# Two graph convolutions on one core: the step loops unrolled, four chunks of edges to a step, the rows of the feature tiles taken in another order

## The reference

```python
deg  = segment_sum(1, src);  dinv = deg > 0 ? rsqrt(max(deg, 1)) : 0
norm = -dinv[src] * dinv[dst]
prop(h)    = segment_sum(h[src] * norm[:, None], dst)
conv(h, l) = h @ Wl_0 + prop(h) @ Wl_1 + bl
h   = leaky_relu(layer_norm(conv(x, 1)) * gamma + beta, 0.01)
out = layer_norm(x + conv(h, 2))
```

## Time and profile before

| | us |
|---|---|
| timed, median of 3 runs (lowest, highest) | 2444.04 (2441.00, 2445.28) |
| profiled execution, span from the first to the last instruction | 3370.7 |
| TensorE busy in it | 2065.1 |
| GpSimd busy | 1700.9 |
| VectorE busy | 1544.4 |
| ScalarE busy | 505.3 |

### The profile page before, as it was taken

How to read it: one execution, slowest core, us unless ns; L and a number is a source line. 1 busy time by engine, 2 the same in 40 slices (tenths; PEclk the granted TensorE clock), 3 DMA queues, 4 the chain that set the end, 5 groups by cost and what they waited for, 6 DMA issues and landing times.

```text
span 3370.7 us, 41016 instructions
## 1 busy us (share of the span) xinstructions
PE 2065.1 (61%) x7250; PEld 963.6 (29%) x7251; DVE 1544.4 (46%) x3507; ACT 505.3 (15%) x1030; POOL 1700.9 (50%) x1725
## 2 busy tenths in 40 slices
PE   6836576665665665665764656565565656555655
PEld 5712232222222322232331222222222222222222
DVE  6754444444444444544443444444444434444444
ACT  5920111111111211111230000000000000000000
POOL 0156554545555554655526545554545445554543
PEclk6558887887887878887876878787777777878778
DMA  6376565655555555655646555565555555555554
GB/s 215 133 259 181 150 174 155 173 159 160 164 167 168 159 165 157 181 159 167 182 132 200 166 158 171 166 177 155 167 159 164 155 158 165 161 165 162 159 159 122
DMA packets 215109, 559.98 MB, mean 166 GB/s; under 512 B 48100, under 2 KB 49760, under 8 KB 214948
## 3 DMA queue, kind: packets, MB, share of 16 engines
q0 software_dynamic: 133120, 436.31, 45.9%
q10 hardware_dynamic: 44676, 81.73, 7.2%
q1 hardware_dynamic: 37152, 40.21, 3.6%
HBM read 493.08 MB, written 64.18 MB: 165 GB/s over the span
## 4 chain that ended last, share of the span: by engine, by line
PE 30%; another core or an unknown queue 26%; issue 25%; DVE 8%; ACT 5%; DVEq 3%; ACTq 1%; DMA 1%; POOL 1%; SPq 0%; POOLq 0%
PE bank L749 16%; PE bank L710 10%; DVE acc L947 6%; PE bank L668 2%; ACT work L556 2%; ACT feat L564 1%; DVEq L923 1%; PE bank L727 1%; PE bank L655 1%; DVEq L947 1%; DVE onehot L923 1%; POOL ring L444 1%; ACT work L546 1%; ACTq L528 0%
## 5 line engine op out<-in xcount | busy, mean ns | idle before, releaser
L444 POOL DMA_INDIRECT ring<-table,index x1664 | 1672.6, 1005 | 1466.5 <-SPq L393 952.1
L947 DVE SCALAR_TENSOR_TENSOR acc<-bank,down,acc 128x512 f32 x928 | 696.9, 751 | 1219.6 <-PE bank L710 709.8
L710 PE MATMUL bank<-ring,onehot 128*128 x3712 | 920.3, 406 | 306.0 <-issue 148.1
L749 PE MATMUL bank<-wA,feat 128*128 128x512 f32 x784 | 547.6, 863 | 804.2 <-ACT feat L564 748.2
L923 DVE TENSOR_SCALAR onehot<-count_h,dst_c,neg_tile 128x128 f16<-128x128 f16 x1856 | 489.2, 329 | 490.1 <-issue 487.6
L710 PEld LDWEIGHTS bank<-ring,onehot 128*128 128x128 f16 x3712 | 380.6, 103 | 865.6 <-issue 515.3
L749 PEld LDWEIGHTS bank<-wA,feat 128*128 128x128 f32 x784 | 212.0, 285 | 1084.9 <-ACT feat L564 774.3
L727 PE MATMUL bank<-wB,base_in 128*128 128x512 f32 x784 | 353.6, 594 | 0.0
L546 ACT ACTIVATE work<-acc 128x512 f32 (+1 forms) x98 | 61.7, 630 | 1747.4 <-issue 1039.3
L727 PEld LDWEIGHTS bank<-wB,base_in 128*128 128x128 f32 x784 | 149.5, 191 | 155.8 <-issue 142.1
L564 ACT ACTIVATE feat<-bank 128x512 f32<-128x512 f32 x98 | 58.5, 597 | 845.4 <-remote 828.7
(11 more groups left out here) (118 smaller groups left out, 689.6 us busy)
## 6 DMA issues: line engine op xcount, KB each, us to landing
ring<-table,index POOLq DMA_INDIRECT x1664
base_in<-feat ACTq DMA_DIRECT2D x98, 256.0 KB
feat<-feat SPq DMA_DIRECT2D x49, 256.0 KB, 2.9
table<-work SPq DMA_DIRECT2D x49, 256.0 KB, 3.1
feat<-feat ACTq DMA_DIRECT2D x49, 256.0 KB
table<-work ACTq DMA_DIRECT2D x49, 256.0 KB
feat<-in_x ACTq DMA_DIRECT2D x48, 256.0 KB
out<-work ACTq DMA_DIRECT2D x48, 256.0 KB
```

The lines of the kernel that those rows point to most:

```text
L444: nc.gpsimd.indirect_dma_start(out=ring[:, at * ROW:(at + 1) * ROW], out_offset=None, in_=table[l], in_offset=bass.IndirectOffsetOnAxis(ap ...
L710: last = nc.tensor.matmul(bank[u % SUM_BANKS][:, :], onehot[:, u, j, :], ring[:, bass.ds(at, D)], start=j + half == 0, stop=j + half == GROUP)
L749: last = nc.tensor.matmul(to[:, :], feat[:, 2 + tile_slot, c * P:(c + 1) * P], wA[:, c * D:(c + 1) * D], start=False, stop=c == KB - 1)
L947: nc.vector.scalar_tensor_tensor(tile_of(acc, tile[u]), bank[u % SUM_BANKS][:, :], col(down[:, l, :], tile[u]), tile_of(acc, tile[u]), ALU ...
```

## The change

- `GROUP` is 4: 208 groups, 208 + 48 = 256 steps a layer with 8 matmuls each. The ring has 4 groups of 4 chunks (the same bytes), and a slot is given back when the group two places earlier is used up and the newer one has landed (`FREE_LAG` 2).
- All loops over steps, groups and gathers are unrolled. GpSimd's gathers lose `bounds_check` and take their indices from one SBUF tensor for the whole layer; the copies of indices by SyncE go.
- The one-hots of two steps (8 matrices) are one `tensor_tensor` with operands repeated by stride 0, from a table `rel` of target minus tile start. `rel` is made in the prologue: 28 comparisons on VectorE (`pick`), 14 fp32 matmuls on TensorE in visits 34 to 47, and an addition. The tables of the steps are built on VectorE behind the first eight low parts rather than behind the last.
- The sums are added unscaled (`tensor_tensor`). The scale is applied by the turn, a matmul of the sums with a scaled identity (`diag`). The copy `staged` goes, and so does the copy of the layer's result back to `acc` in layer 1.
- A visit on TensorE is in another order: first the turns of older tiles, then the dense part of the tile before (`W0`, bias, `W1`), then the turn of its own sums. The lags are 1, 2 and 3. Visits stand behind single steps, about 5.2 steps apart; VectorE's are 3 steps later.
- The load of `W1` (layer 1) moves from the start to behind the picks.

```diff
-    GROUP = 2
-    GROUPS = -(-E // (GROUP * P))
+    GROUP = 4
+    GROUPS = -(-E // (2 * P)) * 2 // GROUP
...
-    RING = UNROLL
-    FREE_LAG = 4
+    BLOCK = 8 // GROUP
+    HOTS = BLOCK * GROUP
+    RING = 16 // GROUP
+    FREE_LAG = RING // 2
...
+    WALK_VISIT = HIST_VISITS + 7
+    PICK_VISIT = HIST_VISITS + 10
...
-    LAG_STATS, LAG_NORMAL, LAG_HIDDEN, LAG_LEAKY, LAG_BACK, LAG_LOW = 1, 2, 3, 4, 5, 6
+    SPACING = STEPS * 256 // TILES
+    FIRST_PLACE = -(-STEPS // TILES) + 8 // GROUP
+    STATS_LATER = -(-STEPS // TILES) // 2
+    LAG_SUMS, LAG_NORMAL, LAG_HIDDEN = 1, 2, 3
...
+                for g in range(GROUPS):
+                    k = g % RING
+                    wait(pool, ring_free, GROUPS * l + g - RING + 1)
+                    for j in range(GROUP):
+                        at = k * GROUP + j
+                        c = g * GROUP + j
+                        nc.gpsimd.indirect_dma_start(
+                            out=ring[:, at * ROW:(at + 1) * ROW], out_offset=None, in_=table[l],
+                            in_offset=bass.IndirectOffsetOnAxis(ap=index[:, c:c + 1], axis=0)
+                        ).then_inc(ring_landed[k], 16)
...
+            def pick_part(m):
+                half, b = m // EDGE_BLOCKS, m % EDGE_BLOCKS
+                at = slice(half * HALF, (half + 1) * HALF)
+                return nc.tensor.matmul(pick_banks[half][:, 0:HALF_COLS].rearrange("p (n j) -> p n j", j=GROUP),
+                                        edge_f[1][:, b * P:(b + 1) * P], pick[b][:, at, :],
+                                        start=b == 0, stop=b == EDGE_BLOCKS - 1)
...
+                if PICK_VISIT <= it.least < PICK_VISIT + 2 * EDGE_BLOCKS:
+                    pe.wait_ge(pick_ready, 1)
+                    last = pick_part(it.least - PICK_VISIT)
...
+            def visit(it, steps, l):
+                if l == 0 and it.within(LAG_NORMAL, TILES + LAG_NORMAL):
+                    k = it.back(LAG_NORMAL)
+                    pe.wait_ge(normed_ready, k.n + 1)
+                    pe.wait_ge(sums_moved, k.n + 2 if k.least + 1 < TILES else TILES)
+                    turn(normed[k.slot], bank[TURN_BANK], normed_turned)
+                if l == 0 and it.within(LAG_HIDDEN, TILES + LAG_HIDDEN):
+                    k = it.back(LAG_HIDDEN)
+                    pe.wait_ge(hidden_ready, k.n + 1)
+                    wait(pe, split1_done, k.n)
+                    turn(feat[:, k.slot, :], bank[BACK_BANK], back_done)
+                if it.within(LAG_SUMS, TILES + LAG_SUMS):
+                    k = it.back(LAG_SUMS)
...
+                    dense(to, base_in[:, k.slot, :], wB, True)
+                    nc.tensor.matmul(to[:, :], ones_b[0:BIAS_PARTS, :], bias_parts[:, l * D:(l + 1) * D],
+                                     start=False, stop=False)
+                    pe.wait_ge(sums_moved, TILES * l + k.n + 1)
+                    dense(to, sums_t[k.slot], wA, False).then_inc(out_done, 1)
+                if it.within(0, TILES):
+                    pe.wait_ge(sums_added, STEPS * l + steps)
+                    pe.wait_ge(diag_ready, TILES * l + it.n + 1)
...
+                    for c in range(KB):
+                        last = nc.tensor.matmul(bank[TURN_BANK][:, c * P:(c + 1) * P],
+                                                acc[:, bass.ds(it.n * D + c * P, P)], diag[:, it.slot, :],
+                                                start=True, stop=True)
+                    last.then_inc(sums_turned, 1)
...
-            looped(dve, low_rows, 0, TILES - 1, 8)
-            straight(low_rows, TILES - 1, TILES, 8)
+            straight(low_rows, 0, 8, 8)
...
+            for b in range(EDGE_BLOCKS):
+                for j in range(GROUP):
+                    last = nc.vector.tensor_scalar(pick[b][:, :, j], group_f, (j - b * P) / GROUP, part_group[:, 0:1],
+                                                   ALU.add, ALU.is_equal)
+            last.then_inc(pick_ready, 1)
...
+            looped(dve, low_rows, 8, TILES - 1, 8)
+            straight(low_rows, TILES - 1, TILES, 8)
...
+                nc.vector.tensor_tensor(onehot[:, b % 2, :, :], count_h[:, :].unsqueeze(1).to_broadcast([P, HOTS, P]),
+                                        rel[:, b * HOTS:(b + 1) * HOTS].unsqueeze(2).to_broadcast([P, HOTS, P]),
+                                        ALU.is_equal).then_inc(onehots_ready, 1)
```

More of the change, by code:

```diff
@@ L276, in load_early, with place, visits_late @@
                 skip_runtime_bounds_check_because="early is a constant less a maximum between zero and it")[1][0]
[L278 to L295, removed]
-            straight(period, 0, 2, 1)
-            looped(eng, period, 2, PERIODS - 1, 1)
-            straight(period, PERIODS - 1, PERIODS, 1)
-        def visits_late(eng, early, drain, visit):
+        def place(v):
+            return min(STEPS, FIRST_PLACE + (v * SPACING >> 8))
+        def visits_late(eng, early, drain, visit, unrolled=False):
             def one(it):
@@ new lines, in _ @@
+            for l in range(2):
+                for n in range(STEPS):
+                    if n % BLOCK == 0:
+                        entry = nc.values_load_multi_w_load_instructions(
+                            step_u[0:1, n * ENTRY:(n + BLOCK) * ENTRY], engines=[mybir.EngineType.PE], min_val=0,
+                            max_val=RING * GROUP * ROW - D, skip_runtime_bounds_check_because=WALK_FITS)[1]
+                    step(l, n, entry[n % BLOCK * ENTRY:(n % BLOCK + 1) * ENTRY])
+                    for v in range(TILES):
+                        if place(v) == n + 1:
+                            with pe.If(early > v):
+                                visit(numbered(v), n + 1, l)
+                visits_late(pe, early, (LAG_HIDDEN, LAG_SUMS)[l], lambda it, steps: visit(it, steps, l), True)
@@ L861, in _ @@
+            assert all(place(v) == FIRST_PLACE + (v * SPACING >> 8) for v in range(BOUNDS)) and place(BOUNDS) == STEPS
+            link(nc.vector.tensor_scalar(place_i[:, 0:1], part_i[:, :], SPACING, None, ALU.mult))
             link(nc.vector.tensor_scalar(place_i[:, 1:2], place_i[:, 0:1], 8, None, ALU.arith_shift_right))
             link(nc.vector.tensor_copy(place_f[:, 0:1], place_i[:, 1:2]))
-            link(nc.vector.tensor_tensor(place_f[:, 1:2], place_f[:, 0:1], part[:, :], ALU.add))
@@ L898, in _ @@
+            for b in range(2):
+                hots(0, b)
             dve.wait_ge(s_bias, 32)
@@ new lines, in visit1 @@
+            def visit1(it, _):
+                if it.within(LAG_NORMAL, TILES + LAG_NORMAL):
+                    shifts(1, it.back(LAG_NORMAL))
+                if it.within(LAG_SUMS, TILES + LAG_SUMS):
+                    k = it.back(LAG_SUMS)
+                    s = k.slot
+                    dve.wait_ge(out_done, TILES + k.n + 1)
+                    dve.wait_ge(s_resid[s], 16 * (k.turn + 1))
+                    nc.vector.tensor_tensor(tile_of(acc, k.n), bank[OUT_BANK + s][:, :], feat[:, 2 + s, :], ALU.add
+                                            ).then_inc(resid_added, 1)
+                    dve.wait_ge(resid_added, k.n + 1)
+                    wait(dve, shift_ready, TILES + k.n - 1 if k.least > 1 else 0)
+                    statistics(1, k.n, s, tile_of(acc, k.n))
```

679 lines of the change are left out of this document (333 added, 346 removed).

## The result

The changed kernel takes 2627.03 us (median of 4 runs, 2626.48 to 2627.96) beside 2444.18 us (4 runs): ratio 1.0753, interval [1.0738, 1.0768]. It is 183 us slower. The forecast was 2470 us, with a range from 2330 to 2560.

The account below looks back on a forecast made before the run. GpSimd's gather issue was taken as the bound from end to end, 2435 us. Adding 12 and 10 (prologue), 2 (between layers) and 8 (end) gave 2467, with part of 9 us left over 2470 us; range 2330 to 2560.

Parts of the forecast that it names:

- What is saved beside the path ... Is the cover there?: VectorE, ScalarE and TensorE work off GpSimd's path: savings worth 0, TensorE keeps up with 18.6 of 22.2 us a tile.
- fourth rival: TensorE becomes the bound, its 18.6 us a tile growing to 23 at a granted clock of 0.8; 2570 us, chance 13%.
- three signs of being wrong: Gathers' distance moves over 0.02 us, GpSimd waits over 30 us for slots, or the first gather comes before 210 us.
- The gathers' distance: GpSimd's 1664 gathers stay 1.305 us apart without the bounds check; 0 us.
- first rival: Gathers get shorter without their check; a twentieth gives 84 us, a tenth 167: 2386 to 2303 us, chance 22%.
- third rival: VectorE's long one-hots hold up GpSimd's gathers, some 70 to 190 us; 2600 us, chance 7%.
- second rival: The recorder is part of the 1.305 us between gathers; at 1.25 us the changed kernel takes 2384 us, chance 12%.
- The stalls belong to the recorded execution: The profile's 914 us of stalls for ring slots are hardly in the timed run, which is GpSimd's issue throughout.
- Between them: From layer 1's last gather to layer 2's first: 40 us against 38, taken as +2 us (-8 to +10).
- VectorE's 12 us: Prologue: picks and table instructions on VectorE make the first gather 12 us late (8 to 16).
- TensorE's 10 us: Prologue: fp32 picks in TensorE's visits, 12 x 0.9 us, add 10 us.
- fifth rival: The prologue hides: ScalarE's slack is larger and TensorE's picks fit in; 2445 us, chance 6%.

Follow-up runs that it names:

- e9: Control: the kernel before with the two counts in its waits written as `max`, on a chip of 2443 us; 2442.93 us, ratio 1.0003.
- e1: The changed kernel with the bounds check put back on its gathers; 2627.46 us, ratio 1.0742.
- e2: The changed kernel with each one-hot built by its own `tensor_scalar` instead of one `tensor_tensor` for eight; 2627.82 us, ratio 1.0746.
- e3: The changed kernel with two numbers a step for TensorE instead of nine, the other offsets added up in registers; 2502.05 us, ratio 1.0236.
- e11: The changed kernel with as many numbers for TensorE, but the offsets as int32 in a load of their own; 2501.7 us, ratio 1.024.
- e10: The kernel before without the bounds check on its gathers, on a chip of 2443 us; 2358.84 us, ratio 0.9656.
- e4: The changed kernel with both one-hots by `tensor_scalar` and two numbers a step for TensorE; 2412.27 us, ratio 0.9876.
- e12: The changed kernel with one-hots by `tensor_scalar`, two numbers a step and the bounds check back, on a chip of 2443 us; 2477.62 us, ratio 1.0144.
- e13: The changed kernel with two numbers a step and one-hots as eight short `tensor_tensor` that keep two tensor inputs; 2428.33 us, ratio 0.9939.
- the second set: Four follow-up kernels run on another chip, where the kernel before itself takes 3455.38 us.
- e8: The changed kernel with one-hots by `tensor_scalar`, two numbers a step and the bounds check back, on the chip of 3455 us; 2761.31 us, ratio 0.799.

## Why the prediction was wrong

**The step that failed** is "What is saved beside the path ... Is the cover there?": the sum by which TensorE needs 18.6 us of 22.2 a tile. It counts matmuls and leaves out the loads of registers, which the change makes from 8 int32 numbers (0.85 us at the median, e9) to 18 uint16 numbers for 16 matmuls (4.26 us). The matmuls' own sum was right: TensorE is busy for 1861 us in the two layers, 19.0 us a tile. In the new kernel two loads with no visit and no wait between them lie 6.30 to 6.34 us apart (the lowest quarter of all distances between loads), where the 16 matmuls take 3.54. So a tile needs 2.61 blocks (a block is two steps with one load) x 6.34 = 16.6 us, and the visit on top. The longest distances are 12.8 to 14.2 us (upper quartile and upper tenth), which puts a visit at 6.5 to 7.9 us and a tile at an estimated 23.8. B / 98 is 23.6. GpSimd needs 21.3 us a tile at 1.250, 22.6 with the gathers that are held up, and 23.1 in e1 with the check. TensorE, or rather its sequencer by my reading of the records, bounds the kernel from end to end, so undoing what slows GpSimd brings nothing (e1, e2), and taking the loads' price away brings 125 us (e3, e11). My fourth rival had the bound and gave it 13%, but by a granted clock of 0.8. The clock is 0.93 in the layers, and 0.93 to 0.94 in e3, which is 125 us faster. The trace of before had the warning: its loads of 8 numbers, 0.59 to 0.87 us each for the middle half. Of the three signs of being wrong two came: the distance moved by 0.055 us, and GpSimd waited 126 us for slots.

**The gathers' distance** ("0 us, the nearest row being the 1.305 us"): wrong, it is 1.250. The first rival had it, at a twentieth; e10 shows 84 us in the kernel before, e4 to e12 65 us in the new one, where other waits take some of it. In the change as made it is worth nothing, since GpSimd isn't the bound (e1).

**The one-hots** (third rival, 70 to 190 us): real, 90 us from e3 to e4, once GpSimd bounds the kernel; nothing before that (e2). Beside one-hots with two tensor inputs 99 gathers are more than 0.1 us over their fellows, beside those with one 17 (e13 against e4). In the changed kernel 235 of the 253 gathers that start during a one-hot end 0.82 us behind its end. What is at work between the two engines no run shows.

**The second rival** (the recorder is part of 1.305) is refuted: in e9 the mean distance is 1.307 us in the profiled execution, which takes 2444.19 us, and the others 2443.

**"The stalls belong to the recorded execution"**: the conclusion was right, that the timed run has none (e9), and the cause wrong. The recorder isn't it, and a chip like that of the second set is the likeliest.

**What was left of the sum** can be read from e12, in which the three are undone, against e9. The first gather: +9.5 us against the 22 foreseen. Within the layers: +5.9 against 0. Between them: +8.9 against +2. The end: +6.7 against +8. Together 31 us against 32, and 2478 us against 2470. That the total fits is luck in part: the prologue was priced too high by 12, and the hand-over and the layers too low by 7 and 6. In the prologue VectorE's 12 us are there (9.5) and TensorE's 10 us are not: the picks hide, as in the fifth rival. ScalarE's visits stay 2.05 us apart in the changed kernel and don't go to 2.9. A stretch of its window view (columns as in the earlier trace rows) and of ScalarE's timeline, with a pick in each visit:

```profile
180.00:190.00 10.00, 7.35 (x31) 3.21 (x30) 7.05 (x10) 8.91 (x16) 5.08 (x10) 1.00 1.01 381
```

```profile
181.56 1.34 ACT L468 ACTIVATE work<-acc,up 128x512 f16 x2 [0.19 <-DMA table<-work]
183.61 1.34 ACT L468 ACTIVATE work<-acc,up 128x512 f16 x2 [0.24 <-DMA table<-work]
```

The granted clock is 1.00 here, where the earlier trace rows has 0.50, and TensorE's timeline shows the two instructions of a pick in 1.02 us and a turn in 0.66:

```profile
181.91 1.02 PE L625 MATMUL bank<-ring,wA 128*128 128x512 f32 x2
183.42 0.66 PE L618 MATMUL bank<-ident,acc 128*128 128x128 f32 x4 [0.49 <-ACT feat L441]
```

With TensorE at 7.35 of 10 us a visit still fits. The 0.9 us a visit behind the forecast's 12 x 0.9 = 10 us is shown by no run: the visits with a pick are as far apart as those of the earlier trace rows, 2.05 us against 187.24 - 185.20 = 2.04. In the changed kernel itself TensorE's lag adds to the last two: C is 56.4 and D 42.1.

## What to carry to other kernels

Count what a sequencer does between two matmuls like any other work: here the loads of registers were on TensorE's path, 4.26 us of 6.3 for two steps, and their price went with the type, 18 uint16 numbers taking 4.26 us and 16 int32 1.11, less than a third for each. When several costs are added at once, only the one at the bound shows; the others are found, like the 90 us here, after it is gone, so edits are to be priced in combination. A wait that the view puts down to one engine can belong to a load that no view lists, so look at what the sequencer did in it. And when a profile and the timed runs differ by nearly 40%, ask whether they come from the same chip before taking the recorder for the cause.

## What the runs showed of the hardware

- Loads of registers from SBUF, by their `TENSOR_LOAD` records (medians). On TensorE: 2 uint16 0.525 us (e11, 256 loads at L748), 4 uint16 0.987 us (e3, L744), 18 uint16 4.26 us (the changed kernel, L744), 16 int32 1.11 us (e11, L745), 8 int32 0.85 us (e9, L699). In the changed kernel also 2 uint16 on VectorE 0.507 us (L1018) and 8 uint16 on SyncE 1.66 us (L359).
- An indirect gather of 128 rows is 0.998 us long on GpSimd with a bounds check (e9), 0.946 without (e10), with 0.30 us to the next in both.
- In the changed kernel 235 of the 253 gathers that start during a `tensor_tensor` one-hot of 1.22 us with two tensor inputs in SBUF are held up and end 0.82 us behind it. None of the 212 that had started first is.
- On the chip of the second set VectorE and ScalarE wait until 723.7 us for matmuls that are recorded at 709.97 and 710.95, with fp32 products behind them (e8). The kernel before takes 3455 us there and 2443 on the others that were used.
